# 192 channels as 128 and 64 rows in the products of q, k, v and MLP one of a four-layer image kernel

## The reference

```python
shortcut = x
xn = layer_norm(x)                     # over 192 channels, then scale and bias
qkv = windows(xn) @ qkv_w + qkv_b      # 192 -> 576
attn = (q * scale) @ k^T + rel_h + rel_w
out = softmax(attn) @ v
x = shortcut + unwindow(out @ proj_w + proj_b)
h = layer_norm(x)                      # over 192 channels, then scale and bias
x = x + gelu(h @ fc1_w + fc1_b) @ fc2_w + fc2_b    # 192 -> 768 -> 192
```

## Time and profile before

| | us |
|---|---|
| median of 3 runs (all: 434.46, 435.51, 436.69) | 435.51 |
| profiled execution: span, first to last instruction | 433.0 |
| profiled execution: its own device time | not listed apart from the span |
| TensorE busy in it | 392.2 (91%) |
| VectorE, ScalarE, GpSimd busy | 217.3, 206.6, 150.7 |
| DMA in it | 17.42 MB in 8425 packets |

### The profile page before, as it was taken

One profiled execution on the slowest core, in us unless ns is written; L12 is line 12 of the kernel. 1 busy time (PEld: TensorE's weight loads), 2 busy tenths in 40 slices (PEclk: granted clock), 3 DMA queues, 4 the chain that ended last, 5 costly groups with the idle time before them and its releaser, 6 DMA issues.

```text
span 433.0 us, 7562 instructions
## 1 busy us (share of the span) xinstructions
PE 392.2 (91%) x2686; PEld 308.4 (71%) x2686; DVE 217.3 (50%) x631; ACT 206.6 (48%) x708; POOL 150.7 (35%) x186
## 2 busy tenths in 40 slices
PE   3599408999999999999999939999999999999997
PEld 1259408888888754886976938888888745986656
DVE  7742105877677760022584318777776720141272
ACT  1142205899988654102115218899899353021220
POOL 9323004776666570000005007776666400000000
PEclk9599957999999999999999979999999999999999
DMA  7989990000000010110002891000000000000002
GB/s 180 87 170 240 158 133 12 2 1 4 1 2 2 2 37 2 54 55 2 0 2 47 162 107 58 3 0 2 2 3 2 2 0 0 2 0 2 0 1 74
DMA packets 8425, 17.42 MB, mean 40 GB/s; under 512 B 1910, under 2 KB 5431, under 8 KB 8387
## 3 DMA queue, kind: packets, MB, share of 16 engines
q1 hardware_dynamic: 8386, 16.93, 21.0%
HBM read 9.68 MB, written 0.79 MB: 24 GB/s over the span
## 4 chain that ended last, share of the span: by engine, by line
PE 85%; DMA 8%; DVE 5%; issue 0%; ACT 0%
PE bank L650 16%; PE bank L726 9%; DMA qaug<-arena 8%; PE bank L679 8%; PE bank L735 7%; PE bank L605 5%; PE bank L704 5%; PE bank L618 5%; PE bank L657 4%; PE bank L656 3%; PE bank L567 2%; PE bank L578 2%; PE bank L895 2%; PE bank L824 2%; PE bank L834 2%; PE bank L748 2%
## 5 line engine op out<-in xcount | busy, mean ns | idle before, releaser
L537 POOL TENSOR_TENSOR probs<-probs,recip 98x392 f32<-98x392 f32 x96 | 80.8, 842 | 34.5 <-DVE recip L1156 33.4
L961 ACT ACTIVATE probs<-bank,negmax 98x196 f32<-98x196 f32 x192 | 80.6, 433 | 9.7 <-DVE negmax L1145 9.3
L650 PE MATMUL bank<-kaug,qaug 100*98 100x196 f32 x384 | 81.1, 334 | 0.0
L1145 DVE TENSOR_REDUCE negmax<-bank 98x2 f32<-98x392 f32 x96 | 53.7, 560 | 22.9 <-PE bank L650 22.9
L650 PEld LDWEIGHTS bank<-kaug,qaug 100*98 100x98 f32 x384 | 55.6, 164 | 7.3 <-ACT probs L961 5.0
L539 POOL TENSOR_SCALAR probs<-probs,recip 112x112 f32<-112x112 f32 (+1 forms) x48 | 28.1, 585 | 68.3 <-DVE recip L1156 66.5
L679 PE MATMUL bank<-ident,probs 98*98 98x98 f32 x384 | 47.5, 247 | 0.2
L656 PE MATMUL bank<-kaug,qaug 100*112 100x112 f32 (+1 forms) x96 | 20.6, 299 | 25.2 <-DMA qaug<-arena 25.2
L679 PEld LDWEIGHTS bank<-ident,probs 98*98 98x98 f32 x384 | 40.1, 127 | 4.2 <-issue 0.5
L726 PE MATMUL bank<-yT,fc 96*128 96x512 f32 x96 | 41.9, 593 | 0.0
L966 ACT ACTIVATE probs<-bank,negmax 112x280 f32<-112x280 f32 (+1 forms) x48 | 24.5, 511 | 35.0 <-DVE negmax L1149 33.5
(11 more groups left out here) (151 smaller groups left out, 600.3 us busy)
## 6 DMA issues: line engine op xcount, KB each, us to landing
fc<-in_fc SPq DMA_DIRECT2D x4, 576.0 KB, 10.3
kaug<-arena SPq DMA_DIRECT2D x6, 346.0 KB, 9.6
qaug<-arena SPq DMA_DIRECT2D x4, 448.0 KB
qaug<-norm_or_q SPq DMA_DIRECT2D x24, 64.0 KB, 2.9
qaug<-arena SPq DMA_DIRECT2D x4, 224.0 KB
qkv<-in_qkv SPq DMA_DIRECT2D x2, 432.0 KB, 11.5
x_tok<-in_x SPq DMA_DIRECT2D x4, 192.0 KB, 3.2
inverse<-in_inverse SPq DMA_DIRECT2D x1, 768.0 KB
```

The costliest lines, as they stand in the source:

```text
L537: pool.tensor_tensor(p, p, by.unsqueeze(2).broadcast_to([n, 2, cols // 2]), ALU.mult).then_inc(s.normed, 1)
L650: last = mm(bank[0:HALF_WIN, 2 * HALF_WIN * part:2 * HALF_WIN * (part + 1)], q[:, at:at + HALF_WIN], keys, start=True, stop=True)
L961: ins = run(m.probs[0:HALF_WIN, slot, cols], bank[0:HALF_WIN, cols], ACT.Exp, bias=m.negmax[0:HALF_WIN, slot, part:part + 1], accum_out=m. ...
L1145: ins = dve.tensor_reduce(m.negmax[0:HALF_WIN, slot], bank[0:HALF_WIN, 0:4 * HALF_WIN].rearrange("k (a n) -> k a n", a=2), AX, ALU.max, ne ...
```

## The change

The 192 channels are laid out as channels 0 to 127 in slot 0 and channels 64 to 191 in slot 1, both with 128 partitions. Channels 64 to 127 thus stand twice, in yT, in yW and in the weights `qkv` and `fc1`. A sum over all 192 is then one product over the 128 rows of one slot, and one over the 64 rows that the other slot has beyond it: rows 64 to 127 of slot 1, or rows 0 to 63 of slot 0. Jobs are taken in pairs. The even one takes slot 0 whole and the rest from slot 1 (rows 64 to 127), the odd one slot 1 whole and the rest from slot 0 (rows 0 to 63). The two whole products are issued first, then the two rests one after the other, into the two banks of the pair, each with its own increment of the semaphore. So both jobs of a pair end together. In the q and k stage the pairs are j = 0 and 1, 2 and 3, 4 and 5; j = 3 is now issued (its 128 rows) before the rest of j = 2. v is paired by images 0 and 1, 2 and 3; the edge job makes whole, rest, whole, rest by itself. The waits stand where they stood.

```diff
+REST = CH - 128
-        m.yT = sb("yT", [HALF, 2, TOKENS])
+        m.yT = sb("yT", [128, 2, TOKENS])
...
+                def rest_rows(n):
+
+                    return slice(REST, 128) if n % 2 == 0 else slice(0, REST)
...
                     if kind == "qk":
-                        for half in range(2):
-                            last = mm(bank[:, :], wl["qkv"][:, half, 128 * g:128 * (g + 1)], m.yT[:, half, 512 * part:512 * (part + 1)],
-                                      start=half == 0, stop=half == 1)
+                        mm(bank[:, :], wl["qkv"][:, j % 2, 128 * g:128 * (g + 1)], m.yT[:, j % 2, 512 * part:512 * (part + 1)], start=True, stop=False)
+                        if j % 2 == 1:
+                            for one in (j - 1, j):
+                                _, chunk, tokens, _ = PROJ[one]
+                                rows = rest_rows(one)
+                                mm(m.bank[4 + one % 4][:, :], wl["qkv"][rows, 1 - one % 2, 128 * chunk:128 * (chunk + 1)],
+                                   m.yT[rows, 1 - one % 2, 512 * tokens:512 * (tokens + 1)], start=False, stop=True).then_inc(s.proj_in.pe, 1)
+                        continue
...
+                        if g == IMAGES:
+                            for tile in range(2):
+                                n, at = EDGE_TOKENS[tile], EDGE_AT[tile]
+                                o = bank[0:n, CH * tile:CH * (tile + 1)]
+                                mm(o, m.yW[:, 0, at:at + n], wl["qkv"][:, 0, 2 * CH:3 * CH], start=True, stop=False)
+                                last = mm(o, m.yW[REST:128, 1, at:at + n], wl["qkv"][REST:128, 1, 2 * CH:3 * CH], start=False, stop=True)
...
                         for tile in range(2):
-                            for half in range(2):
-                                last = mm(bank[0:n, CH * tile:CH * (tile + 1)], m.yW[:, half, at:at + n], wl["qkv"][:, half, 2 * CH:3 * CH],
-                                          start=half == 0, stop=half == 1)
+                            at = HALF_WIN * (2 * g + tile)
+                            mm(bank[0:HALF_WIN, CH * tile:CH * (tile + 1)], m.yW[:, g % 2, at:at + HALF_WIN], wl["qkv"][:, g % 2, 2 * CH:3 * CH],
+                               start=tile == 0, stop=False, skip_group_check=True)
+                        if g % 2 == 1:
+                            for tile in range(2):
+                                for one in (g - 1, g):
+                                    at, rows = HALF_WIN * (2 * one + tile), rest_rows(one)
+                                    last = mm(m.bank[4 + (j - (one != g)) % 4][0:HALF_WIN, CH * tile:CH * (tile + 1)], m.yW[rows, 1 - one % 2, at:at + HALF_WIN],
+                                              wl["qkv"][rows, 1 - one % 2, 2 * CH:3 * CH], start=False, stop=True, skip_group_check=True)
...
-                    for half in range(2):
-                        last = mm(m.bank[j % 4][:, :], wl["fc1"][:, half, 128 * hid:128 * (hid + 1)], m.yT[:, half, 512 * g:512 * (g + 1)],
-                                  start=half == 0, stop=half == 1)
-                    last.then_inc(s.fc1.pe, 1)
+                    mm(m.bank[j % 4][:, :], wl["fc1"][:, j % 2, 128 * hid:128 * (hid + 1)], m.yT[:, j % 2, 512 * g:512 * (g + 1)], start=True, stop=False)
+                    if j % 2 == 1:
+                        for one in (j - 1, j):
+                            rows, at = rest_rows(one), 128 * (one % HID_TILES)
+                            mm(m.bank[one % 4][:, :], wl["fc1"][rows, 1 - one % 2, at:at + 128], m.yT[rows, 1 - one % 2, 512 * g:512 * (g + 1)],
+                               start=False, stop=True).then_inc(s.fc1.pe, 1)
...
-        out[f"qkv{l}"] = g("qkv_w").reshape(2, HALF, 3 * CH).transpose(1, 0, 2)
+        out[f"qkv{l}"] = _split(g("qkv_w"))
...
-        out[f"fc1{l}"] = g("fc1_w").reshape(2, HALF, HID).transpose(1, 0, 2)
+        out[f"fc1{l}"] = _split(g("fc1_w"))
```

More of the change, by code:

```diff
@@ L249, in build @@
         m.spare = sb("spare", [128, 2])
-        m.yW = m.probsT[0:HALF].rearrange("p a n -> p (a n)")[:, 0:2 * TOKENS].rearrange("p (a n) -> p a n", a=2)
+        m.yW = m.probsT[:].rearrange("p a n -> p (a n)")[:, 0:2 * TOKENS].rearrange("p (a n) -> p a n", a=2)
         arena = sb("arena", [128, QK_CHUNKS * KEYS + 4 * TOKENS])
@@ L566, in turn_norm @@
                     for half in range(2):
-                        last = nc.tensor.transpose(m.bank[bank0 + 2 * g + half][0:HALF, 128 * i:128 * (i + 1)],
-                                                   m.xn[:, 4 * g + i, HALF * half:HALF * (half + 1)], c["ident"][:])
+                        last = nc.tensor.transpose(m.bank[bank0 + 2 * g + half][:, 128 * i:128 * (i + 1)],
+                                                   m.xn[:, 4 * g + i, REST * half:REST * half + 128], c["ident"][:])
                         if i == 3:
@@ L624, in attention @@
                         pe.wait_ge(s.y_ordered, 2)
-                        for tile in range(2):
-                            n = HALF_WIN if g < IMAGES else EDGE_TOKENS[tile]
-                            at = HALF_WIN * (2 * g + tile) if g < IMAGES else EDGE_AT[tile]
-                            for half in range(2):
-                                last = mm(bank[0:n, CH * tile:CH * (tile + 1)], m.yW[:, half, at:at + n], wl["qkv"][:, half, 2 * CH:3 * CH],
-                                          start=half == 0, stop=half == 1)
+                        if g == IMAGES:
[4 more added lines that the diff above has]
+                                last = mm(o, m.yW[REST:128, 1, at:at + n], wl["qkv"][REST:128, 1, 2 * CH:3 * CH], start=False, stop=True)
+                            last.then_inc(s.proj_in.pe, 1)
+                            continue
+                        for tile in range(2):
+                            at = HALF_WIN * (2 * g + tile)
[7 more added lines that the diff above has]
+                                              wl["qkv"][rows, 1 - one % 2, 2 * CH:3 * CH], start=False, stop=True, skip_group_check=True)
+                                    if tile == 1:
+                                        last.then_inc(s.proj_in.pe, 1)
+                        continue
                     last.then_inc(s.proj_in.pe, 1)
@@ L919, in take_norm @@
                 act.wait_ge(ln.pe, 2 * g + 1)
-                run(m.yT[:, 0, 512 * g:512 * (g + 1)], m.bank[bank0 + 2 * g][0:HALF, :], ACT.Identity,
-                    scale=wl["vecs"][0:HALF, col:col + 1], bias=wl["vecs"][0:HALF, col + 2:col + 3]).then_inc(ln.act, 1)
+                run(m.yT[:, 0, 512 * g:512 * (g + 1)], m.bank[bank0 + 2 * g][:, :], ACT.Identity,
+                    scale=wl["vecs"][:, col:col + 1], bias=wl["vecs"][:, col + 2:col + 3]).then_inc(ln.act, 1)
             def attention(l):
@@ L1072, in take_norm @@
                     dve.wait_ge(ln.pe, 2 * g + 2)
-                    dve.tensor_scalar(m.yT[:, 1, 512 * g:512 * (g + 1)], m.bank[bank0 + 2 * g + 1][0:HALF, :],
-                                      wl["vecs"][0:HALF, col + 1:col + 2], wl["vecs"][0:HALF, col + 3:col + 4], ALU.mult, ALU.add).then_inc(ln.dve, 1)
+                    dve.tensor_scalar(m.yT[:, 1, 512 * g:512 * (g + 1)], m.bank[bank0 + 2 * g + 1][:, :],
+                                      wl["vecs"][:, col + 1:col + 2], wl["vecs"][:, col + 3:col + 4], ALU.mult, ALU.add).then_inc(ln.dve, 1)
                 for g in range(2):
@@ L1291, in _halves, with _split @@
     return v.reshape(2, HALF).T
+def _split(v):
+    return np.stack([v[:128], v[REST:]], 1)
 def _block_diagonal(blocks):
@@ L1311, in _laid_out @@
         for at, v in ((0, g(s1)), (2, g(b1)), (4 + QK_CHUNKS, g(s2)), (6 + QK_CHUNKS, g(b2))):
-            vecs[:HALF, at:at + 2] = _halves(v)
+            vecs[:, at:at + 2] = _split(v)
         vecs[:, 4:4 + QK_CHUNKS] = np.concatenate([qb, kb]).reshape(QK_CHUNKS, 128).T
         out[f"vecs{l}"] = vecs
-        out[f"qkv{l}"] = g("qkv_w").reshape(2, HALF, 3 * CH).transpose(1, 0, 2)
+        out[f"qkv{l}"] = _split(g("qkv_w"))
         for heads in REL_HEADS:
```

## The result

The changed kernel took **430.03 us** (median of 14 runs, 427.45 to 433.66) against 435.04 us (14 runs, 432.12 to 436.75) of the kernel before on the same chip: a ratio of 0.9897, 95% interval 0.9871 to 0.9922. That is 4.5 us (3.4 to 5.6) less, where the sum had 3.5. The profiled execution's span is 428.1 us, before 433.0. By the bound of 0.5% it is faster, as forecast, and 2.0 us under the predicted 432.0; 0.5 us of that is the start, which the prediction took from three runs as 435.5.

A forecast was written before the change was run, and what follows sets the result against it. TensorE was taken to bound MLP one, and the position-term DMA transfers the q, k, v stage. Terms -2.15 - 2.45 - 0.65 + 1.8 = -3.45 us took 435.5 to 432.0 us, range 429.0 to 437.5.

The forecast's parts named there:

- A pair of products: Two neighbouring products on TensorE: 3.43 us become 3.00 with full overlap and 0.42 for mode changes, saving 0.43 us.
- The two rivals on the overlap: The pair's short products overlap by one pass only (3.43 us per pair, chance 0.09) or not at all (chance 0.08).
- the second rival: No overlap on row halves in each pair's last two products: 0.44 us lost per pair, 7.7 us in all; chance 0.08.
- MLP one: Six pairs per layer, the first limited by VectorE's normalise: 2.15 us saved in layer 0, 2.45 in layer 1.
- q and k of layer 1: SyncE can begin the copies into qaug 0.65 us earlier: 0.43 + 0.43 - 0.2 from the first two pairs.
- VectorE's normalise lets the last tile through in time: First q, k pair of layer 1: normalise ends at 226.04, so the transposes follow at once and the full 0.43 us counts.
- a new wait of 0.2 us at most: Second q, k pair of layer 1: j = 3 may wait for ScalarE's eviction of part 1, at most 0.2 us.
- v: v products: pairs save about 0.3 us each, edge windows pay four changes of about 0.18; sum near zero, under the transfer wait.
- The loads: Larger qkv and fc1 weights on layer 0's full DMA queue: 1.8 us later, bounds 0 to 3.1.
- what is put ahead pushes these back: Layer 0 DMA queue: bytes loaded ahead delay the position terms, 0.83 us for 147 KB and 0.96 for 197 KB.
- The sign for layer 1: New profile: first score product of layer 1 to come 1.0 us earlier than before, 256.9 for 257.86.
- The third rival: Loads cost 3.1 us and mode changes 0.1 us more than taken: net under 1 us, 434.7 us, no change; chance 0.07.

The follow-up runs named there:

- q, k, v alone: Only q, k, v changed (weights, first norm, products) against the kernel before, MLP one left at two products of 96 rows: 434.88 us, ratio 0.9984.
- the loads alone: Kernel before with the qkv and fc1 weights zero-padded to 128 rows, products still using 96: 434.75 us against 435.57, ratio 1.0001.
- 786 KB: Kernel before with one more load of 786 KB queued behind those of MLP one and two, into an unused place: 437.08 us, ratio 1.0043.

## Why the prediction was right, and where it was off

**A pair of products: right.** 2.97 us measured for 3.00; two changes 0.39 us for 0.42, and the run that takes changes out has the same 0.2 for one. The price read from the column quarters of the bursts, with the wider weight load added, held for halves of the rows. Without the part added it would have been 0.31; that it is the weight load is likely, since none ran ahead over a change, and was not tested by itself.

**The two rivals on the overlap fell.** One pass of overlap would show 3.43 us per pair, no overlap 3.87; the trace has 2.97. With the rests on the same rows it has 3.82, so the second rival's price was right, and its case did not occur. (By the prediction's own terms it is 3.85 us for 3.43, a loss of 0.42; the 3.87 and 0.44 there are a slip that moves the rival by 0.2 us.) The Trainium skill, TensorE: Matmul & The Clock Gate, section Part 3, has matmuls strictly in order in start and end. The four weight loads within 0.30 us and the four records within 1.13 us do not fit it if each pass is a place in that order: the second product's first pass did not wait for the first product's second. With whole products as the places they would; no run here decides how the order counts.

**MLP one: right, a little low.** Layer 0: 2.15 forecast, 2.29 measured; layer 1: 2.45 and 2.53, both with the last change of mode that shows in MLP two. With the measured pair, five pairs give 5 x (3.43 - 2.97) = 2.3, plus in layer 1 what the first pair can bring. That is set by VectorE's normalise as expected: transposes and first four products took 3.46 + 0.87, now 1.73 + 1.06 + 1.30 = 4.09, 0.24 us for the 0.3 taken. In layer 0 the normalise covers the first pair, again as forecast.

**q and k of layer 1: 0.65 forecast, 0.47 measured.** Two steps were off.

The first is "VectorE's normalise lets the last tile through in time". In the first pair TensorE won 3.44 - 2.78 = 0.66 us, and the transposes behind it grew from 0.87 to 1.32. The last two transposes follow the end of the normalise by 0.48 us (157.93 + 0.44 - 157.89 in layer 0). In the kernel before they could end at 226.04 + 0.48 = 226.52, and ended at 226.74: only 0.22 us was there to be had. After, that normalise ends at 222.32 + 1.25 = 223.57, and the transposes 0.51 us behind it. So this pair brought 0.21 of the 0.43 us.

The second is "a new wait of 0.2 us at most". It came from VectorE's half of yT, not from ScalarE's, and cost 0.36 us: TensorE stood for 0.12 us from 224.94, when the two passes of j = 2 were through, to 225.06, and then took 1.10 us for the two passes of j = 3 instead of 0.86, since their weight loads had waited too. The timeline has the four passes at 2.26 us. Counted so, it is over the 0.3 us that the prediction named as a sign of being wrong. The pair still brought 0.30 us (3.13 for 3.43) where 0.23 was forecast, because its first product stands behind transposes and pays no change of mode, which the forecast had charged.

Together 0.51 us, of which 0.47 reached SyncE. From there to the first score product the profiles scatter by 1.5 us (24.6 to 26.1), with and without the change, so no single profile shows it, nor does the time of q, k, v alone.

**v: right.** The v products took 6.74 us in layer 0 before and 6.73 after. The position products ahead of them grew from 10.39 to 10.57 us in layer 1, one change of mode, and all of it is under the transfer.

**The loads: wrong, and the main error.** The term was +1.8 us, with 0 to 3.1 as its bounds; the loads alone measured 0.0 (-1.2 to +1.3). It failed at "what is put ahead pushes these back", which takes every byte ahead of the position terms at full price. Even 786 KB cost half of that. A second misreading stood under it: the 66.55 us of the profiled execution was taken as the kernel's own, while a second profile of the same kernel had 63.98. A shift of 1.8 us could not have been seen against that in one profile. Without the term the sum is -5.25 us; measured are -4.5 us (-5.6 to -3.4). So the forecast time came out as near as it did in part by two errors against each other: 1.8 us of loads that cost nothing measurable, and 0.65 us from q and k that no time shows. The sign for layer 1 says the same: its first score product was to come 1.0 us earlier and came 2.5 us earlier (255.35 for 257.86). In the table that is MLP one's 2.40, while the other five differences ahead of it nearly cancel (-1.26, +1.08, +0.12, -0.47, +0.42); the +1.08, from the lower clock, was not in the forecast.

**The third rival,** the loads at their dearest and costly changes, fell with both its parts.

## What to carry to other kernels

Here a sum of 192 rows as 128 + 64 paid only because two of the short products ran at once on different row halves (0.85 us per pair; on the same rows the kernel lost 1.3%), and each change between full and half rows cost 0.2 us: order the work so that neighbours share a mode. Where the next stage begins with transposes of freshly normalised tiles, work out first how much that other engine leaves to be had: here the first pair of three stages gave 0, 0.24 and 0.21 us in place of 0.46. The price per byte on a full DMA queue was an upper bound. A landing time from one profile is one draw of several, and a start that comes earlier behind a long idle stretch can be eaten by the time at the lower clock: cut the whole span into stages, so that the differences add up to the measured one.

## What the runs showed of the hardware that was not expected

- Behind a load of 97 rows the next issue held SyncE for 11.4 to 15.6 us in the profiles with it, and for 0.31 us behind the same load as 96 rows and one, with issues of 4.78 and 3.80 us later in its place. The Trainium skill, DMA: Bandwidth & Descriptors, section "Why a DMA increments its semaphore by 16 and not by 1", has a transfer spread over the largest number of engines up to 16 that divides its rows: 96 rows take 16, 97 take one. The trace agrees as far as the stall goes, which left with the split; how many engines a load used, no run here shows.
- Issuing the position terms 2.8 us earlier did not bring the landing earlier (66.11 against 65.29 us), and that moment differs by 2.6 us between two profiles of one kernel whose MLP one stages agree within 0.01 us.
- Over a change between full and half rows no weight load ran ahead (0.76 us without any); within the full rows they did (161.62 and 162.04, while the passes before were still under way).
- Behind a long idle stretch TensorE ran its scores at half the clock for 3.61 to 6.69 us, and the stretch from the first score product of layer 0 to MLP one grew with that time, by 1.27 us (86.82 to 88.09) over those 3.08.
